# Attention and deformable convolution on one core: the order of TensorE's three groups inside a unit

## The reference

```
x1  = x + attention(group_norm(x))        # channel attention: softmax of q k^T over channels
x2  = group_norm(x1)
off = clip(conv3x3(x2, off_w) + off_b)     # two offsets for each pixel and tap
msk = 2 * sigmoid(conv3x3(x2, mask_w) + mask_b)
y   = deform_conv(x2, off, msk, proj_w) + proj_b
out = x1 + gelu(batch_norm(y))             # statistics over all 32 images
```

## Time and profile before

| | us |
|---|---|
| median of 3 runs | 4188.26 |
| lowest and highest run | 4175.98, 4193.26 |
| the profiled execution | 4178.93 |
| its span, first to last instruction | 4177.2 |

### The profile page before, as it was taken

One profiled execution on the slowest core, in us unless ns is written; L12 is line 12 of the kernel. 1 busy time (PEld: TensorE's weight loads), 2 busy tenths in 40 slices (PEclk: granted clock), 3 DMA queues, 4 the chain that ended last, 5 costly groups with the idle time before them and its releaser, 6 DMA issues.

```text
span 4177.2 us, 109865 instructions
## 1 busy us (share of the span) xinstructions
PE 3611.8 (86%) x38338; PEld 3084.8 (74%) x38338; DVE 2654.0 (64%) x5834; ACT 2110.4 (51%) x4790; POOL 1412.7 (34%) x1165
## 2 busy tenths in 40 slices
PE   3999999999999899999999999899999999999800
PEld 2777877878787787878778787777887778778700
DVE  3666766666667666666766666676666666666522
ACT  1545555555555455555545555554555455455422
POOL 1333333333333333333333333333333333333311
PEclk8999999999999999999999999999999999999955
DMA  2000000000000000000000000000000000000199
GB/s 61 19 17 20 28 28 20 27 27 27 10 28 28 21 27 27 27 11 27 28 20 27 28 28 10 28 28 20 27 28 27 10 28 28 28 20 17 46 367 328
DMA packets 50912, 172.07 MB, mean 41 GB/s; under 512 B 9664, under 2 KB 10880, under 8 KB 50176
## 3 DMA queue, kind: packets, MB, share of 16 engines
q1 hardware_dynamic: 39584, 136.75, 10.7%
q0 software_dynamic: 7168, 25.17, 1.5%
q10 hardware_dynamic: 3424, 0.90, 0.1%
HBM read 87.29 MB, written 75.50 MB: 39 GB/s over the span
## 4 chain that ended last, share of the span: by engine, by line
PE 64%; DVE 13%; issue 11%; ACT 4%; DMA 4%; DVEq 2%; ACTq 1%; SPq 1%; POOL 0%; POOLq 0%
PE sps L652 10%; PE acc L669 6%; PE acc L670 6%; PE acc L671 6%; PE l L580 4%; PE zps L638 3%; DVE zl L1138 3%; PE zps L642 3%; PE zps L639 3%; PE zps L640 3%; PE zps L641 3%; DMA xn<-x_scratch 2%; DVE sl L1144 2%; DVE ych L1206 2%; PE l L512 2%
## 5 line engine op out<-in xcount | busy, mean ns | idle before, releaser
L1325 POOL TENSOR_TENSOR sT<-ay,bx 128x768 f32<-128x768 f32 x768 | 1149.5, 1507 | 1530.0 <-PE sps L652 1461.2
L1144 DVE TENSOR_TENSOR sl<-sps,sh 128x384 f16<-128x384 f32 x1536 | 846.7, 551 | 662.8 <-ACT sh L889 658.5
L889 ACT CAST sh<-sps 128x384 f16<-128x384 f32 x1536 | 741.2, 483 | 831.9 <-PE sps L652 822.7
L670 PE MATMUL acc<-zl,sh 128*128 128x192 f16 x4608 | 1149.4, 249 | 3.4 <-issue 3.4
L669 PE MATMUL acc<-zh,sh 128*128 128x192 f16 x4608 | 1149.6, 249 | 0.3 <-ACT ypm L912 0.3
L671 PE MATMUL acc<-zh,sl 128*128 128x192 f16 x4608 | 1149.4, 249 | 0.0
L652 PE MATMUL sps<-eye,sT 128*128 128x128 f32 x4608 | 801.9, 284 | 239.9 <-issue 136.0
L855 ACT CAST zh<-zps 128x288 f16<-128x288 f32 x1536 | 620.4, 404 | 685.6 <-PE zps L642 659.9
L1138 DVE TENSOR_TENSOR zl<-zps,zh 128x288 f16<-128x288 f32 x1536 | 693.5, 452 | 406.2 <-ACT zh L855 401.2
L652 PEld LDWEIGHTS sps<-eye,sT 128*128 128x128 f32 x4608 | 542.1, 143 | 393.1 <-issue 170.7
L670 PEld LDWEIGHTS acc<-zl,sh 128*128 128x128 f16 x4608 | 457.8, 99 | 24.4 <-issue 4.4
(11 more groups left out here) (200 smaller groups left out, 6498.0 us busy)
## 6 DMA issues: line engine op xcount, KB each, us to landing
xin<-in_x SPq DMA_DIRECT2D x32, 512.0 KB, 5.3
xin<-in_x SPq DMA_DIRECT2D x64, 256.0 KB, 5.8
x_scratch<-x SPq DMA_DIRECT2D x32, 512.0 KB, 2.7
y_scratch<-ych SPq DMA_DIRECT2D x32, 512.0 KB, 2.7
zh<-y_scratch SPq DMA_DIRECT2D x20, 512.0 KB, 11.2
zl<-x_scratch SPq DMA_DIRECT2D x20, 512.0 KB, 12.7
out<-zh POOLq DMA_DIRECT2D x20, 512.0 KB, 8.7
x_scratch<-x SPq DMA_DIRECT2D x32, 256.0 KB, 3.4
```

Source lines behind the costliest of these rows:

```text
L670: pe.matmul(acc[:, 0:C], s_h, zl[:, j, ky, z], start=False, stop=False)
L889: act.copy(sh[:, u % S_RING].rearrange("p k n -> p (k n)"), sps[u % 2][:, 0:3 * P]).then_inc(s_hi, 1)
L1144: dve.tensor_tensor(one(sl), sps[u % 2][:, 0:3 * P], one(sh), ALU.subtract).then_inc(s_lo, 1)
L1325: pool.tensor_tensor(sT[:, p % ST_RING].rearrange("p k (r x) -> p k r x", r=R), a, x_, ALU.mult)\
```

## The change

Inside a unit of TensorE the z group is written ahead of the products of S and z. The transposes stay first and `turn_y` and `part0` stay last. `offset_max` in unit 9 stays right behind the products. The programs of the other engines are not touched, and no instruction is added or removed.

```
@@ -738,13 +738,13 @@
                         turn_s(u + 2, b)
                     elif more:
                         turn_s(u + 2 - UNITS, b + 1)
-                    convolve(u, b, par)
-                    if u == 9:
-                        offset_max(b)
                     if u + AHEAD < UNITS:
                         z_group(u + AHEAD, b, par)
                     elif more:
                         z_group(u + AHEAD - UNITS, b + 1, 1 - par)
+                    convolve(u, b, par)
+                    if u == 9:
+                        offset_max(b)
                     if u % 12 == 2 and u > 12:
                         turn_y(u // 12 - 1, b)
                     if more:
```

## The result

The change makes the kernel 1.8% slower.

A forecast was written before the change was run, and what follows sets the result against it. TensorE bounds the kernel: its own work, busy 86% of the span, plus its waits. Terms of 1.79 us an image, times 31, add 55 us to the profiled 4178.9, giving 4234; forecast median 4244 us, range 4202 to 4262.

The forecast's parts named there:

- Unit 38: Z still waits for VectorE's last `move` copy, C now runs behind it: +0.74 us an image.
- Units 40 to 44: VectorE's `ay` of unit 41 newly waits behind GpSimd's `sT`, delaying T of unit 44: +0.70 us an image.
- The rival of the shrinking stalls: Earlier `zl` passed on in full shortens stalls ahead of units 11 to 44: 4148 us, chance 0.08.
- The image end: `turn_y(3)` stays 1.60 us behind C's first product, and Z no longer fills that time: +0.61 us an image.
- Unit 28: Earlier `zl` lets the moments, and line 503 waiting for them, come earlier: -0.26 us an image.
- units 10 and 21: Softmax step (21) and a residue (10) stay held by GpSimd's `sT`: 0, bounds -0.71 and -0.18 us.
- T's load behind C: T's weight load behind C's shorter product costs nothing; as a rival it sticks out: 4282 us, chance 0.03.
- The sum: 0.61 + 0.74 + 0.70 - 0.26 = 1.79 us an image, times 31 is 55 us.
- nor did anything cancel: Rival: VectorE isn't held by GpSimd but the later `ypm` counts, +0.04 us an image: 4190 us, chance 0.18.
- The clock: Slower granted clock after the image end's idle time: nothing, at most +0.5 us an image (+15 us).

The follow-up runs named there:

- undo_41: The changed kernel with unit 41 alone back in its old order (C ahead of Z): 4244.47 us, ratio 1.0138 to the kernel before.
- undo_47: The changed kernel with unit 47 alone back in its old order (C ahead of Z): 4240.18 us, ratio 1.0144 to the kernel before.
- fill_38: The changed kernel with 13 unused identity products on TensorE between T and Z's wait in unit 38: 4236.29 us, ratio 1.0136 to the kernel before.
- only_38: The kernel before the change, with Z ahead of C in unit 38 alone: 4238.9 us, ratio 1.0125.
- bx_last: The changed kernel with GpSimd's `bx` of the next image made in unit 43, behind the last `sT`, not 41: 4240.78 us, ratio 1.0128 to the kernel before.
- undo_38: The changed kernel with unit 38 alone back in its old order (C ahead of Z): 4219.47 us, ratio 1.0088 to the kernel before.
- three_undone: The changed kernel with units 38, 41 and 47 back in their old order: 4153.84 us, ratio 0.992 to the kernel before.
- best_of: three_undone with GpSimd's `bx` also moved from unit 41 to 43, behind the last `sT`: 4157.13 us, ratio 0.994 to the kernel before.
- two_only: The kernel before the change, with Z ahead of C in units 27 and 40 alone: 4153.36 us, ratio 0.9928.
- before_act: The kernel before the change, with the softmax's last step on ScalarE instead of VectorE: 4173.88 us, ratio 0.998.
- three_act: three_undone with the softmax's last step on ScalarE instead of VectorE: 4151.16 us, ratio 0.9909 to the kernel before.

## Why the prediction was right and wrong

**Unit 38, forecast +0.74.** Right, +0.74. The copies of `move` didn't move: the residue of unit 32 started 0.6 us earlier, 0.27 us behind the start of `sT`, took 2.29 us in place of 1.71, and ended 1.08 us behind the end of `sT`, as before:

```profile
2181.57 2.29 DVE L1001 TENSOR_TENSOR x_lo_a<-xn,x_hi_a 128x1024 f16<-128x1024 f32 x1
```

```profile
2181.30 1.48 POOL L1325 TENSOR_TENSOR sT<-ay,bx 128x768 f32<-128x768 f32 x1 [0.72 <-PE sps L652]
```

That is the rule of the Trainium skill that the prediction weighed (SBUF — State Buffer, "SBUF: two separate sides"), and the trace agrees. The prediction saw one such place in that row of work. There are two more, before and after alike: the first two copies of line 1010 each start behind an `sT`, end 0.05 us after it and take 1.45 us, where the third takes 0.17.

**Units 40 to 44, forecast +0.70.** Right in size, +0.71, and right that `ay` meets `sT`. It was put down to the later `zh` of unit 41, and undo_41 bears that out: with `zh` early the collision goes. What I didn't see is how close the race is. `ay` was to start 0.6 to 0.9 us behind `sT`, it started 0.37 behind, and ahead by 0.06 it costs nothing; so the same earlier `off` that does harm with unit 41 changed is a gain with unit 41 as it was, some 20 us over the images. The rival of the shrinking stalls had 0.74 us for this place, but with unit 41 changed; that the order of this one unit turns the gain into a loss, neither the forecast nor a rival had.

**The image end, forecast +0.61.** Right: `turn_y(3)` stays 1.60 us behind C, and undo_47 gave the 0.61 us back in every image.

**Unit 28, -0.26, and units 10 and 21, nothing.** Right: -0.27; the softmax step started 0.04 us behind `sT` where 0.05 had been worked out.

**T's load behind C, nothing.** Right: T stays 0.74 us behind C's first product in a plain unit, as in the earlier trace rows.

**The sum.** The terms gave 55 us, and 55 us is what the steps show. The stalls didn't shrink elsewhere, nor did anything cancel.

**The clock: this step failed.** The prediction had "I put nothing on it, and up to +0.5 an image". It looked for the clock only where TensorE already stood longest, at the end of the image, and asked what 0.6 us more would do there: 4 us (the first three units of an image take 7.61 us on average after, 7.48 before). The new wait in unit 38 was priced as 0.74 us of idle time, and nothing else. But it falls in a stretch in which TensorE had just stood 1.07 us; together they brought the granted clock to 1.2 GHz in 15 of 31 images, 1.63 us each. The term of unit 38 was mis-sized: not 0.74 but 0.74 + 0.8 us an image. fill_38 shows the second part apart from the first.

## What to carry to other kernels

Price a new wait of the engine that bounds the kernel twice: by its length, and by what the engine did in the microseconds ahead of it. A wait of 0.8 us behind one of 1.1 us cost double here, and a few products without a purpose in it, 0.9 us of them, took 26 of its 43 us away. And an order is worth changing only in the units where a wait hangs on it: two of 48 held the gain (0.7%), three held the loss (1.8% with them), the rest nothing.

## What of the hardware was not expected

**The clock falls behind two waits of about a microsecond, with three transposes between them.** Where unit 38 has both waits, the granted clock fell to 1.2 GHz in 15 images of after, 9 of undo_47, 23 of undo_41, 20 of only_38 and 21 of bx_last; where it has the first alone, or the second filled, in none (before, undo_38, fill_38, and the five kernels with unit 38 in its old order: three_undone, best_of, two_only, before_act and three_act). Each of the 88 falls begins 1.25 to 2.35 us behind T of unit 38; the second wait ends 1.32 us behind it. The same waits to within 0.01 us fell in one image and not in the next, so length alone doesn't decide. What else does is open.

**The clock takes back gains.** undo_41, bx_last and three_act turned less of their shorter waits into time than expected: 41, 30 and 26 us of waits for 18, 21 and 3 us between the medians (the 3 us are no more than noise). In undo_41 and bx_last the falls in unit 38 became more frequent; in three_act the slow stretch at the image start became longer. Why is open in both.

**A start of 0.06 us decides who waits, VectorE or GpSimd.** `ay` ahead of `sT` by 0.06 us: `ay` takes 0.45 us and `sT` 1.74 (0.03 to 0.06 us in all 31 images of undo_41 and of three_undone). Behind it by 0.37 us: `ay` takes 1.42 us and `sT` 1.48.
